# Inverse roots of the dense pipeline on ScalarE and VectorE in place of two GpSimd powers a tick

## The reference, cut to what matters

```python
x = _layernorm(x + L0(x, edge_index))   # hypergraph convolution, twice, with PReLU
x = _layernorm(x + L1(x, src, dst))     # GATv2 attention, 8 heads
x = _layernorm(x + L2(x, edge_index))   # GAT, 4 heads of 32, projected to 256
x = _layernorm(x + L3(x, edge_index))   # GAT, 4 heads of 64, relu, divided by its row norm
```

```python
def _layernorm(x, axis=-1, eps=1e-05):
    m = jnp.mean(x, axis=axis, keepdims=True)
    v = jnp.var(x, axis=axis, keepdims=True)
    return (x - m) / jnp.sqrt(v + eps)
```

## Time and profile before

| | |
|---|---|
| median of 3 executions | 7682.7 us (7667.08 to 7689.8) |
| the profiled execution | 7685.41 us, span 7683.6 us |
| PE busy | 5978.5 us (78%), mean granted clock 0.822 |
| DVE busy | 4799.3 us (62%) |
| ACT busy | 3220.5 us (42%) |
| POOL busy | 3957.0 us (51%) |
| POOL line 2007, 104 powers of 12 numbers | 240.1 us, 2309 ns each |
| POOL line 2016, 104 powers of 8 numbers | 176.5 us, 1697 ns each |

### The profile page before, as it was taken

One profiled execution on the slowest core, in us unless ns is written; L12 is line 12 of the kernel. 1 busy time (PEld: TensorE's weight loads), 2 busy tenths in 40 slices (PEclk: granted clock), 3 DMA queues, 4 the chain that ended last, 5 costly groups with the idle time before them and its releaser, 6 DMA issues. The chain is left out here.

```text
span 7683.6 us, 97926 instructions
## 1 busy us (share of the span) xinstructions
PE 5978.5 (78%) x26448; PEld 4443.4 (58%) x26448; DVE 4799.3 (62%) x12659; ACT 3220.5 (42%) x8521; POOL 3957.0 (51%) x3334
## 2 busy tenths in 40 slices
PE   6887878777779999998887767888868888644554
PEld 4555555555556677676666555666656777433332
DVE  5544455555455555667878766777766666577776
ACT  2433334554455555775444333333323333222222
POOL 6666667666553332555555644555543233255554
PEclk8888988888889999999998887777767877655555
DMA  1111113444343333665444534444433434333332
GB/s 40 35 35 33 37 34 107 137 135 140 125 161 127 128 128 115 209 216 179 163 151 150 178 134 134 138 141 137 141 109 120 136 131 135 104 106 106 104 107 76
DMA packets 380609, 926.13 MB, mean 121 GB/s; under 512 B 85192, under 2 KB 158771, under 8 KB 380070
## 3 DMA queue, kind: packets, MB, share of 16 engines
q1 hardware_dynamic: 271078, 702.94, 26.2%
q0 software_dynamic: 108992, 216.92, 10.0%
HBM read 568.90 MB, written 361.35 MB: 121 GB/s over the span
## 5 line engine op out<-in xcount | busy, mean ns | idle before, releaser
L2019 POOL DMA_INDIRECT got<-hop,end_i x600 | 632.2, 1054 | 674.4 <-PE psum L949 491.6
L2019 POOL DMA_INDIRECT got<-tab,end_i x600 | 647.0, 1078 | 448.5 <-PE psum L1056 270.3
L1056 PE MATMUL psum<-got,sf 128*128 128x264 f32 (+2 forms) x1200 | 482.4, 493 | 488.9 <-DVE got L1752 394.7
L949 PE MATMUL psum<-got,sf 128*128 128x256 f32 x1600 | 535.6, 419 | 210.0 <-ACT got L1183 168.7
L1984 POOL DMA_INDIRECT recs<-rec_x,pos x586 | 581.8, 993 | 206.6 <-issue 177.4
L1056 PEld LDWEIGHTS psum<-got,sf 128*128 128x128 f32 x1200 | 236.5, 242 | 557.4 <-DVE got L1752 439.9
L949 PEld LDWEIGHTS psum<-got,sf 128*128 128x128 f32 x1600 | 306.1, 206 | 371.2 <-issue 254.1
L1221 ACT ACTIVATE res<-res,l_mo 128x256 f32<-128x256 f32 x600 | 312.1, 591 | 489.4 <-DVE l_mo L1654 489.2
L2007 POOL TENSOR_TENSOR d_rs<-d_sums,power 128x12 f32<-128x12 f32 x104 | 240.1, 2309 | 486.8 <-DVE d_sums L1585 482.7
L1183 ACT COPY got<-psum 1x256 f32<-1x256 f32 x796 | 283.4, 356 | 487.2 <-PE psum L949 350.2
L858 PE MATMUL psum<-wd,t2t 128*128 128x256 f32 x1568 | 396.5, 398 | 46.2 <-DVE h_t L1521 45.8
(11 more groups left out here) (363 smaller groups left out, 16205.4 us busy)
## 6 DMA issues: line engine op xcount, KB each, us to landing
own<-hop SPq DMA_DIRECT2D x150, 512.0 KB
x_t<-res SPq DMA_DIRECT2D x150, 512.0 KB
xo<-x_t SPq DMA_DIRECT2D x150, 512.0 KB
hop<-res SPq DMA_DIRECT2D x100, 512.0 KB
x_in<-in_x SPq DMA_DIRECT2D x98, 512.0 KB
out<-hd SPq DMA_DIRECT2D x98, 512.0 KB
tab<-tab SPq DMA_DIRECT2D x50, 536.0 KB
own<-tab SPq DMA_DIRECT2D x50, 536.0 KB
```

What stands on the lines that cost most here:

```text
L949: T.matmul(o, sf_of(q)[:, k * P:(k + 1) * P], got_of(q)[:, k * FEAT:(k + 1) * FEAT], start=(p < 3), stop=True).then_inc(at("l_agg"), 1)
L1056: T.matmul(bank(3 + k % 2)[:, 0:g.ext], sf_[:, k * P:(k + 1) * P], got_of(q)[:, k * g.width:k * g.width + g.ext], start=True, stop=True).t ...
L2019: eng.indirect_dma_start(out=dst, out_offset=None, in_=table, in_offset=bass.IndirectOffsetOnAxis(ap=idx, axis=0), bounds_check=rows_ - 1, ...
```

## The change

GpSimd's two powers of a tick are taken out. In their place ScalarE takes, over all 20 numbers of the tick in one tile `d_v` (12 sums and 8 variances), the logarithm and then the exponential of -0.5 times it (part `root`), and VectorE makes one Newton step for y = v^-0.5 from it (y times (1.5 - 0.5 v y y), three operations at the head of `ratio`). `shd` becomes the fourth operation of `ratio`. The 20 numbers are now one result that waits for both `sums` and `mo` of the tick before; every reader of `d_rm` or `d_rs` now waits for `ratio`. ScalarE's table set is named once at the start. The planner gets `root` with length 0.5 and `ratio` with 1.4 in place of 0.6, and since GpSimd has no dense part any more and the lengths differ, it makes a new order for all engines.

```diff
@@ dense_parts
-        add(("V", "sums", t), 0.35, [..., ("G", "pows", t - 2), ...])
-        add(("G", "pows", t), 2.3, [("V", "sums", t)])
-        add(("V", "ratio", t), 0.6, [("G", "pows", t), ("V", "ud", t - 6), ("V", "mo", t - 1)])
+        add(("V", "sums", t), 0.35, [..., ("S", "root", t - 2), ...])
+        add(("S", "root", t), 0.5, [("V", "sums", t), ("V", "mo", t - 1)])
+        add(("V", "ratio", t), 1.4, [("S", "root", t), ("V", "ud", t - 6), ("V", "mo", t - 1), ("S", "ln", t - 7)])
...
-        add(("V", "mo", t), 1.0, [..., ("V", "shd", t), ("G", "powm", t - 1), ("V", "t21", t - 2)])
-        add(("G", "powm", t), 1.7, [("V", "mo", t - 1), ("S", "ln", t - 7)])
-        add(("V", "shd", t), 0.2, [("G", "powm", t), ("S", "ln", t - 7), ("V", "mo", t - 1)])
+        add(("V", "mo", t), 1.0, [..., ("V", "ratio", t), ("V", "t21", t - 2)])
...
-            add(("V", "t2", d), 0.96, [("T", f"l1{c}", d), ("G", "powm", d + 1), ...], h=c)
+            add(("V", "t2", d), 0.96, [("T", f"l1{c}", d), ("V", "ratio", d + 1), ...], h=c)
@@ scalar_dense
+            elif name == "root":
+                eng.wait_ge(at("d_sums"), d + 2)
+                if d >= 0:
+                    eng.wait_ge(at("d_h"), 3 * (d + 1))
+                S.activation(d_i[:, d % 2], d_v[:, d % 2], ACT.Ln).then_inc(at("d_lg"), 1)
+                eng.wait_ge(at("d_lg"), d + 2)
+                S.activation(d_rr[:, d % 2], d_i[:, d % 2], ACT.Exp, scale=-0.5).then_inc(at("d_rr"), 1)
@@ scalar_program
+            eng.preload_act_table_set("natural_log_exp_and_others")
@@ vector_tick, ratio
-                eng.wait_ge(at("d_rs"), t + 2)
+                eng.wait_ge(at("d_rr"), t + 2)
...
+                root = d_rr[:, t % 2]
+                V.tensor_tensor(d_w[:, 0], root, d_v[:, t % 2], ALU.mult).then_inc(at("d_nw"), 1)
+                eng.wait_ge(at("d_nw"), 2 * (t + 1) + 1)
+                V.scalar_tensor_tensor(d_w[:, 1], d_w[:, 0], -0.5, root, ALU.mult, ALU.mult).then_inc(at("d_nw"), 1)
+                eng.wait_ge(at("d_nw"), 2 * (t + 1) + 2)
+                V.scalar_tensor_tensor(d_r[:, t % 2], d_w[:, 1], 1.5, root, ALU.add, ALU.mult).then_inc(at("d_rs"), 1)
+                eng.wait_ge(at("d_rs"), t + 2)
+                V.scalar_tensor_tensor(d_sh[:, t % 2, :], d_mo[:, K:2 * K, 0], -0.5, d_rm[:, t % 2, 1, :], ALU.mult, ALU.mult).then_inc(at("d_sh"), 1)
@@ gpsimd
-        def gpsimd_dense(eng, name, t):
-            if name == "pows":
-                eng.wait_ge(at("d_sums"), t + 2)
-                G.tensor_tensor(d_rs[:, t % 2]..., d_sums[:, t % 2]..., power[:, 0:3 * K], ALU.pow).then_inc(at("d_rs"), 1)
-            else:
...
-                G.tensor_tensor(d_rm[:, t % 2]..., d_var[:, t % 2, :], power[:, 0:2 * K], ALU.pow).then_inc(at("d_rm"), 1)
```

More of the change, by code:

```diff
@@ L138, in dense_parts @@
 def dense_parts(plan, nd):
-    late = {"x": -0.6, "xt": -0.6, "w1": 0.0, "rx": 0.1, "h": 0.1, "w2": 0.2, "nr": 0.0, "yb": 0.0, "bn": 0.0, "mo": 0.0, "pows": -0.5, "powm": -0.5, "ratio": -0.4, "sums": -0.5,
-            "shd": -0.4, "y1r": 0.5, "bny": 0.5, "l1": 1.0, "t2": 1.0, "sq2": 1.5, "t2t": 1.5, "l2": 2.0, "t3": 2.0, "sq3": 2.5, "t3t": 2.5, "l3": 3.0, "hd": 3.0,
+    late = {"x": -0.6, "xt": -0.6, "w1": 0.0, "rx": 0.1, "h": 0.1, "w2": 0.2, "nr": 0.0, "yb": 0.0, "bn": 0.0, "mo": 0.0, "root": -0.5, "ratio": -0.4, "sums": -0.5,
+            "y1r": 0.5, "bny": 0.5, "l1": 1.0, "t2": 1.0, "sq2": 1.5, "t2t": 1.5, "l2": 2.0, "t3": 2.0, "sq3": 2.5, "t3t": 2.5, "l3": 3.0, "hd": 3.0,
             "rl": 3.0, "sqn": 3.0, "ud": 4.0, "ln": 5.0, "dst": 5.0, "xin": 0.0}
@@ L510, in build_program @@
         ident0 = sb("ident0", [P, P])
-        power = sb("power", [P, 12])
+        power = sb("power", [P, K])
         w1 = sb("w1", [P, 2, FEAT])
@@ L556, in build_program @@
         d_acc = sb("d_acc", [P, 3, K])
-        d_sums = sb("d_sums", [P, 2, 3, K])
-        d_rs = sb("d_rs", [P, 2, 3, K])
-        d_var = sb("d_var", [P, 2, 2 * K])
-        d_rm = sb("d_rm", [P, 2, 2, K])
+        d_v, d_i, d_rr, d_r = (sb(t, [P, 2, 5 * K]) for t in ("d_v", "d_i", "d_rr", "d_r"))
+        d_w = sb("d_w", [P, 2, 5 * K])
+        d_sums = d_v[:, :, 0:3 * K].rearrange("p t (s k) -> p t s k", s=3)
+        d_var = d_v[:, :, 3 * K:5 * K]
+        d_rs = d_r[:, :, 0:3 * K].rearrange("p t (s k) -> p t s k", s=3)
+        d_rm = d_r[:, :, 3 * K:5 * K].rearrange("p t (s k) -> p t s k", s=2)
         d_sh = sb("d_sh", [P, 2, K])
@@ L670, in build_program @@
         dense_names = {"x0", "x1", "w10", "w11", "w20", "w21", "y1r0", "y1r1", "bny0", "bny1", "l10", "l11", "l20", "l21", "l30", "l31", "t2t0", "t2t1", "t3t0", "t3t1",
-                       "xt0", "xt1", "rx0", "rx1", "h0", "h1", "nr0", "nr1", "yb0", "yb1", "yb", "bn", "mo", "sums", "pows", "powm", "ratio", "shd", "t20", "t21", "t30", "t31",
+                       "xt0", "xt1", "rx0", "rx1", "h0", "h1", "nr0", "nr1", "yb0", "yb1", "yb", "bn", "mo", "sums", "root", "ratio", "t20", "t21", "t30", "t31",
                        "sq2", "sq3", "hd0", "hd1", "rl0", "rl1", "sqn", "ud", "ln", "xin", "dst"}
@@ L1362, in vector_prep @@
             V.memset(d_mo[:], 0.0)
-            V.memset(d_var[:], 1.0)
-            V.memset(d_sums[:], 1.0)
+            V.memset(d_v[:], 1.0)
             V.memset(d_sd[:], 1.0)
@@ L1605, in vector_tick @@
                 V.memset(d_mo[:, 0:1, 3], 0.0).then_inc(at("d_bns"), 1)
-            elif name == "mo":
+            else:
                 st = d_bn[:].rearrange("p s k m -> p (s k) m")
@@ L2119, in gpsimd_program @@
                     gpsimd_patch(eng, part[1])
-                elif part[0] in dense_names:
-                    gpsimd_dense(eng, *part)
                 else:
```

39 lines of the change are left out of this document (11 added, 28 removed).

## The result

The changed kernel takes 8137.5 us in the median of four executions (8132.85 to 8155.45), against 7684.7 us for the kernel before: a ratio of 1.0598, with a 95% interval of 1.0574 to 1.0621. It is 6% slower, where 7430 us were forecast. The profiled execution of after took 8138.54 us.

What follows compares the result with a forecast made beforehand. TensorE bounds passes 1 and 2; in scatter and pass 0 GpSimd's powers tie its DMAs to the dense pace. From 7685.4 us, -213 - 224 + 52 + 64 + 55 + 8 = -258 gives 7430 us, range 7240 to 7600.

Steps and rivals of the forecast that it cites:

- with the same pace of ticks everything behind moves forward by 195 us: Scatter stretch: index tables come after 29 sums, not 35, at an unchanged tick pace; main part of -213 us.
- Pass 0: Dense work of 23.7 ticks at 36.1 us each, 856 us where 1080 were measured before: -224 us.
- the 36.1 us for a tick: Pass 0: TensorE busy 26.1 + 3.3 = 29.4 us a tick, plus the 6.7 idle of a scatter tick.
- the floor of 760: Pass 0: lower bound from GpSimd, 560 DMAs x 1.32 = 739 us, with about 20 us at the boundary.
- Passes 1 to 4: Dense ticks moved into later passes: pass 1 +52 us, pass 2 0, pass 3 +64, pass 4 +55.
- The new operations: Logarithm, exponential and Newton step: 0 in the tick-bound stretches, 0.6 x 14 = +8 us in pass 3.
- The dearest case: Every tick: ScalarE's pair, a hop each way and the Newton chain lie open, some 2.3 us.
- The freer loop: Rival: unhooked GpSimd keeps TensorE at full clock; pass 0 -96, scatter ticks 3.5 us shorter (-98); 7240 us, chance 0.13.
- The root lies open: Rival: the root path costs 2.3 us a tick in scatter and pass 0, +122; 7550 us, chance 0.11.
- only moved: Rival: 11.7 ticks come back at full 32.8 us and new operations cost more; 7694 us, same, chance 0.05.
- Starved TensorE: Rival: late root makes TensorE wait for PSUM banks in scatter and pass 0, 5.5 us a tick; 7722 us, chance 0.08.
- The port: Rival: the powers had blocked VectorE, so 53 ticks gain 4.0 us more each; 7218 us, chance 0.03.

Runs made afterwards that it cites:

- chip D: Before and after run unchanged on another chip, where TensorE's results are not read late: 7261.3 and 7126.7 us, ratio 0.9815.
- the first experiment: Kernel after with one idle GpSimd power of 12 numbers (2.3 us) after every 8 scatters of the preparation: 7665.4 us.
- chips C, D and E: The three chips without late TensorE signals; the kernel before took 7273, 7261 and 7255 us there.

## Why the prediction was wrong, point by point

**What bounds the kernel** was read half right. GpSimd's queue was tied to the dense pace, and the ties cost what was said. But the 6.7 us of TensorE's idle time in a tick and the wait of 154.4 us for the carried row were taken for the dense pipeline's and the gathers' own. On chip D the kernel before has ticks of 27 us in the scatter, 24.0 of them busy on TensorE and 2.9 idle, and a pass 0 of 875 us, not 1080: much of both was already the lag. TensorE's waits for the carried row in pass 0, first of before on chip D, then of after in the result:

```profile
PE psum L949 <- ACT got L1183: 58.1, 46, 4.4
```

```profile
PE psum L950 <- ACT got L1191: 179.6, 52, 19.1
```

So the wait didn't go with the powers (154.4 with them, 179.6 without). It goes with the chip: in after on chip D it is 69.2 us.

**The step that failed** is "with the same pace of ticks everything behind moves forward by 195 us". GpSimd's part of it was nearly right (the last scatter ends at 830 for 793). The pace of the dense ticks was taken as independent of what GpSimd does; it went from one tick in 32.8 us to one in 182 with the last pause gone, and the first gather came at 1539 us where 1010 was forecast. The text even asked what stands behind the waits in GpSimd's queue, but not what the silence of that queue gave to others. The trace of before has it, some us behind the last row, and the prediction doesn't read it. A burst of scatters ends at 467.1, and 2.3 us later ScalarE and VectorE start together; VectorE, idle for 6.2 us by then, reads there the product that TensorE had started at 459.14 and ended at 461.03, 8.4 us before:

```profile
466.16 0.97 POOL L1984 DMA_INDIRECT recs<-rec_x,pos  x1 [0.30 <-issue]
...
469.42 0.69 ACT L1105 ACTIVATE y1t<-psum,nb 128x512 f32<-128x512 f32 x1 [4.39 <-remote]
469.44 0.87 DVE L1554 SCALAR_TENSOR_TENSOR t3d<-psum,d_rs,bc 128x256 f32<-128x256 f32 x2 [6.21 <-remote]
```

Taken over the whole trace of before, the lag of ScalarE's reads grows with the number of indirect DMAs in the 20 us before the product's end: 0.04 us up to 7 of them, a mean of 0.5 at 10 and 11, 3.2 at 12 and 13, 4.7 at 14 and 15. That curve would have warned of a loss, not told its size: the unbroken stream has 15 or 16 in 20 us, hardly more than its last point, and a median lag of 14.1.

**Pass 0** (-224, measured -3): with the lag, 24 ticks take as long as 29 did, so the step that failed is the 36.1 us for a tick, which again took the pace of the dense pipeline as its own; measured are 1077/24 = 44.9. Without the lag pass 0 takes 759 us on chip D, which is the floor of 760 that the prediction gave. That the missing powers are what made the lag costlier here is argued, not shown: runs of gathers had a median of 12 DMAs in before and in after.

**Passes 1 to 4** (+179 with the new operations, measured +137): held, but for pass 3. The moved ticks cost what the rows of before gave: +35 and +60 for forecast +52 and +55. Pass 3 was priced too dear (+24 for +72).

**The new operations** (+8): held; ticks of 25.0 us contain them, and no stretch shows a cost. The dearest case, 2.3 us, holds some 1.1 us for two hops between engines that no row gave; the trace shows 0.03 us from ScalarE's exponential to VectorE.

**The rivals.** The freer loop (7240) is what happens, in kind, on the chips without the lag: ticks of 25.0 us in the scatter and pass 0 at its floor. "The root lies open" and "only moved" did not happen. "Starved TensorE" (7722) had the right victim, but a price of 5.5 us a tick where 149 (182 - 32.8) were paid, and the wrong cause: TensorE did not starve behind the root. "The port" is out: on chips C, D and E ticks of the scatter take 25.0 us with 36 to 73 powers beside them and without any.

**The forecast by stretch, on chip D** (from before to after there): scatter -147 for -213, pass 0 -116 for -224, pass 1 +38 for +52, pass 2 +8 for 0, pass 3 +19 for +72, pass 4 +57 for +55; together -141 us in the profiled executions (7263.4 to 7122.0) and -135 in the medians. The two large gains were forecast too large for this chip since their base held the lag: its kernel before has them in part already (1049 and 875 us for 1221 and 1080).

**A version that beats both** was not found where the lag exists. The pauses of the first experiment in the scatter (7665) and the short ones in pass 0 (898 for 1090 us) were not run in one kernel; their sum would be 7665 - 192 = 7473, an estimate. Where there is no lag, the kernel after is the best of all that ran.

## What to carry to other kernels

Before a helper's work is taken out of an engine's queue, ask what the pauses in that queue gave to the others, not only who waited for it; look in the trace of before for results that are read late although the reader was idle, and for instructions of one group that drift apart with nothing to wait for, and set them against what another engine issues at that time. Here a stop of 1.1 us after every 4 indirect DMAs kept TensorE's signals on time (in pass 0), one of 2.3 us after every 8 nearly did (in the scatter, ticks of 29.6 us for 25.0), and a memset after every 8 did not. And take the kernel before to a second chip: a change that gains 1.9% on one can lose 6% on another, and only the trace of before on both tells how much of its idle time is the program's.

## What the runs showed of the hardware

- On two of five chips an unbroken stream of indirect DMAs on GpSimd (one each 1.3 us) delays TensorE: matmuls of one product come apart by up to 2.8 us (3.5 in the result) from about the 13th DMA of a burst on, and results are read 14 us late in the median, 36 at most. The DMA queue was 2.5% busy. On three chips neither occurs. Why, no run shows.
- The kernel before is 5.6 to 5.9% slower on the two chips (7684 and 7682 against 7255 to 7273 us). Of the 420 us between the trace ahead of the prediction and that of chip D, 172 are in the scatter stretch and 205 in pass 0; the passes from 1 on differ by 3 to 15 us each.
- ScalarE and VectorE hand over to each other without such a lag in the same stretch: 0.03 us from the exponential to the Newton step in each tick looked at.
